# A cross-attention and fp4 feed-forward kernel: the down projection as three f32r products in place of one f32 product

## Chip, cores and metric

One core of a Trainium2 chip runs the whole program. The metric is the device time of one execution in microseconds (us), lower is better. A second number for the same execution is the span of its trace, from the first to the last instruction of the program.

## What is computed

For x (8, 512, 256) and ctx (8, 512, 256): layer norm, cross-attention with 16 heads of 16 and an additive bias and mask, a residual, then layer norm and a feed-forward of width 704 whose activations and weights are all rounded to fp4 in blocks of 16, and a residual. The change is in the last product.

```python
def fp4_quant_dequant(x):                       # blocks of 16 along the last dim
    scale = jnp.max(jnp.abs(xb), axis=-1, keepdims=True) / 6.0
    q = _GRID[jnp.searchsorted(_MID, jnp.abs(xb / scale))] * jnp.sign(xb) * scale

def fp4_linear(x, w):
    return jnp.einsum('bsk,nk->bsn', fp4_quant_dequant(x), fp4_quant_dequant(w))

x = x + attention(layernorm(x), ctx, ctx, bias, mask)
x2 = layernorm(x)
gate, y = fp4_linear(x2, w_gate), fp4_linear(x2, w_up)
h = jax.nn.silu(gate) * y
out = x + fp4_linear(h, w_down)                 # (4096, 704) times (704, 256)
```

## The kernel before

The program is written by hand, engine by engine: each of the blocks `sync`, `gpsimd`, `scalar`, `vector` and `tensor` is the instruction stream of one engine, and the streams meet only at counted semaphores. No scheduler moves anything, so an instruction waits for its semaphore and for all that stands before it on its engine.

**Attention, about 25 to 690 us.** The outer loop runs over 8 batch elements, each in 32 steps (`S_`). A step makes two score tiles of 128 x 512 (`scores`, L1331). VectorE takes each one from PSUM, adds the bias and finds the row's maximum in one instruction (`less_scores`, L1089), and writes it to `prob`, a ring of 13 buffers (`RING`). GpSimd or ScalarE subtracts the maximum (`less_max`). TensorE transposes the tile four steps later (`T_LAG`, 8 tiles), ScalarE takes the exponential, and TensorE multiplies by the values. Between the tiles lie the projections of the next octet of heads, and, in the last batch element, the nine pieces in which the feed-forward weights are made: VectorE, GpSimd and ScalarE round a piece, TensorE transposes it (`make_weights`), ScalarE copies it to SBUF (`take_weights`, L764 to L767 for w_down). For gate and up the copy goes to an f32r buffer `w_gu_high`, and VectorE stores what the rounding to f32r lost in `w_gu_low` (`weights_low`, L1031). For w_down the copy goes to an f32 buffer `w_dnT`, and `weights_low` returns without doing anything.

**Feed-forward, about 690 to 929 us.** 32 row tiles of 128 rows go through a software pipeline (`ffn_step` on each engine, iteration n). In iteration n TensorE does, in this order: the six transposes of the rounded h of tile n-3 into `ps_h` (L1233 by way of the helper `transposes`); the gate and up products of tile n (L1567 to L1569, three f32r products for each of two chunks and three column ranges, 18 in all); two transposes of the rounded x of tile n+1 into `ps_x` (L1578), which leave the accumulation open; the first three chunks of the down product of tile n-3 (L1584); one product of minus the identity with the high part of x (`neg_ident`, L1594), which leaves x minus its high part in `ps_x`; and the last three chunks of the down product. The down product has six chunks of the 704 (padded to 768) rows of h, stationary `f_hqT` and moving `w_dnT`, both f32; each `matmul` call appears in the trace as two MATMUL records.

ScalarE does in iteration n: the copy of `ps_h` to `f_hqT` for tile n-3 (L903), two steps of the normalisation of tile n+3 (L874, L878), silu of tile n (L909), an absolute value for x of tile n+2 (L896), the high part of x of tile n+1 (`x_high`, L884), an absolute value for h of tile n-1 (L918), and the low part of x of tile n+1 (`x_low`, L889).

VectorE does the rounding steps and the last addition (L1197), and GpSimd scales the rounded h (L701).

Of the kernel before, what the change touches and what calls it, by code (L numbers as in the profile page):

```python
# [21 lines left out]
P = 128  # L22
# [19 lines left out]
def xattn_ffn(nc, x, ctx, bias, mask, w_in, b_in, w_out, b_out, w_gate, w_up, w_down, out):  # L42
# [19 lines left out]
    TILES = 2 * STEPS  # L62
    T_LAG = 4
    V_LAG = 8
    RING = 13
    VW = D + 1

    x_v = x.rearrange("b (t p) e -> p (b t) e", p=P)
# [5 lines left out]
    with cx:  # L74
        def sb(name, shape, dt=F32):
            return cx.enter_context(nc.sbuf_tensor(name, shape, dt))

        def sem(name):
            return cx.enter_context(nc.semaphore(name))
# [5 lines left out]
        eps_t = sb("eps_t", [P, NT])  # L85
        neg_half = sb("neg_half", [P, NT])

        att = sb("att", [P, 28352])
        used = [0]

        def cut(*shape):
            n = 1
            for s in shape:
                n *= s
            a = att[:, used[0]:used[0] + n]
            used[0] += n
            assert used[0] <= att.shape[1], used[0]
            names = "abcd"[:len(shape)]
            if len(shape) == 1:
                return a  # L100
            return a.rearrange(f"p ({' '.join(names)}) -> p {' '.join(names)}",
                               **{k: s for k, s in zip(names[1:], shape[1:])})
# [16 lines left out]
        O_sb = cut(S)  # L119
        O_n = cut(NT, E)  # L120
        oT = cut(EC, S)
        at_w_dn = used[0]
        w_dnT = cut(IC, E)
        w_outT = cut(EC, E)
        bv_bc = cut(E)
        bo_bc = cut(E)


        w_qT = att[:, at_w_dn:at_w_dn + EC * E].rearrange("p (c e) -> p c e", c=EC)

        w_nat = probT.rearrange("p a b c d -> p (a b c d)")[:, 0:8 * E].rearrange("p (c e) -> p c e", c=8)

# [27 lines left out]
        kv_hl = sb("kv_hl", [P, 4 * EC * S], F32R)  # L160
        ctxT_high, ctxT_low, w_kv_high, w_kv_low = (
            kv_hl[:, i * EC * S:(i + 1) * EC * S].rearrange("p (c s) -> p c s", c=EC) for i in range(4))
        assert 2 * E == S and EC * GU <= 4 * EC * S
        w_gu_low = kv_hl[:, 0:EC * GU].rearrange("p (c n) -> p c n", c=EC)

        WPC = 512
# [27 lines left out]
        def lows_of(z):  # L194


            return sum(1 for i in range(z) if piece_rows(i)[0] < 2)
        used[0] = at_bias
        f_xc = cut(E)
        f_xn = cut(2, E)  # L200
# [13 lines left out]
        f_hu = cut(I)  # L214

        f_hq = cut(2, IC * P)
        f_hqT = cut(2, IC, P)
        f_out = cut(2, E)
        assert used[0] <= at_bias

        psum = cx.enter_context(nc.psum_tensor("psum", [P, 8, 512], F32))
        ps_score, ps_O = psum[:, 0:3, :], psum[:, 6, :]
# [58 lines left out]
        fhy_ready, fha_ready = sem("fhy_ready"), sem("fha_ready")  # L281
        fhu_ready, fhd_ready, fhq_ready = sem("fhu_ready"), sem("fhd_ready"), sem("fhq_ready")
        fhT_ready, fhT_taken = sem("fhT_ready"), sem("fhT_taken")
        fdn_ready, fout_ready = sem("fdn_ready"), sem("fout_ready")
        stored = [sem(f"stored{i}") for i in range(2)]

# [273 lines left out]
        def _(pool):  # L560
# [77 lines left out]
            for o in range(EC):  # L638
                pool.memset(vv[:, o, :, 0:8 * VW].rearrange("p c (h m) -> p c h m", m=VW)[:, :, :, D:VW], 1.0).then_inc(vv_zero, 1)

            pool.memset(w_dnT[:, IC - 1, :], 0.0).then_inc(vv_zero, 1)
            low_k(0)
            low_q(0)
            for tt in range(NT):
# [63 lines left out]
        def _(act):  # L708
# [44 lines left out]
            def take_weights(z, bank):  # L753

                act.wait_ge(gwT_ready, z + 1)
                src = bank.rearrange("p (c n) -> p c n", c=2)
                g, m = piece_rows(z)
                if g < 2:

                    act.wait_ge(score_ready, TILES * (N_OCT - 1))  # L760
                    cols = min(2 * P, I - m * P)
                    act.activation(w_gu_high[:, :, g * I + m * P:g * I + m * P + cols], src[:, :, 0:cols], ACT.Copy).then_inc(gwT_taken, 1)
                elif m < IC - 2:
                    act.activation(w_dnT[:, m:m + 2, :], src, ACT.Copy).then_inc(gwT_taken, 1)  # L764
                else:
                    act.activation(w_dnT[:, m, :], src[:, 0, :], ACT.Copy)
                    act.activation(w_dnT[0:ILAST, m + 1, :], src[0:ILAST, 1, :], ACT.Copy).then_inc(gwT_taken, 1)  # L767

            def exp_tile(n, s, r):

# [127 lines left out]
            def ffn_step(n, par):  # L898
                m = n - 3
                if live(m):  # L900
                    act.wait_ge(fhT_ready, m + 1)
                    wait(act, fdn_ready, m - 1)
                    act.activation(f_hqT[:, 1 - par, :, :].rearrange("p c t -> p (c t)"), ps_h[:, 0:IC * P], ACT.Copy).then_inc(fhT_taken, 1)  # L903
                x_norm(n + 3, 1 - par)
                m = n
                if live(m):
                    act.wait_ge(fgate_ready, m + 1)
                    wait(act, fh_ready, m - 1)
                    act.activation(f_sil[:, par, :], ps_gu[:, 0:I], ACT.Silu).then_inc(fsil_ready, 1)  # L909
                if live(n + 2):  # L910
                    x_abs(n + 2, par)
                if live(n + 1):
                    x_high(n + 1, 1 - par)
                m = n - 1
                if live(m):
                    act.wait_ge(fhy_ready, m + 1)
                    wait(act, fhd_ready, m)
                    act.activation(f_ha, f_hy[:, 1 - par, :], ACT.Abs, scale=PULL).then_inc(fha_ready, 1)  # L918
                if live(n + 1):
                    x_low(n + 1, 1 - par)  # L920
            batches(act, body)
# [20 lines left out]
        def _(dve):  # L942
# [288 lines left out]
        def _(pe):  # L1231
# [317 lines left out]
            def ffn_step(n, par):  # L1549
                m = n - 3  # L1550
                if live(m):
                    if isinstance(m, int) and m == 0:
                        pe.wait_ge(o_taken, 2 * B)
                    pe.wait_ge(fhq_ready, m + 1)
                    wait(pe, fhT_taken, m)
                    for c in range(IC):
                        last = transposes(ps_h[:, c * P:(c + 1) * P], f_hq[:, 1 - par, c * P:(c + 1) * P])
                    last.then_inc(fhT_ready, 1)
                m = n
                if live(m):  # L1560
                    pe.wait_ge(fxlow_ready, m + 1)
                    wait(pe, fh_ready, m)
                    for c0 in range(0, GU, 512):
                        c1 = min(c0 + 512, GU)

                        for c in range(EC):
                            pe.matmul(ps_gu[:, c0:c1], f_xqT_high[:, par, c, :], w_gu_high[:, c, c0:c1], start=c == 0, stop=False)  # L1567
                            pe.matmul(ps_gu[:, c0:c1], f_xqT_high[:, par, c, :], w_gu_low[:, c, c0:c1], start=False, stop=False)  # L1568
                            last = pe.matmul(ps_gu[:, c0:c1], f_xqT_low[:, par, c, :], w_gu_high[:, c, c0:c1], start=False, stop=c == EC - 1)  # L1569
                        if c0 < I <= c1:  # L1570
                            last.then_inc(fgate_ready, 1)
                    last.then_inc(fgu_ready, 1)
                m = n + 1
                if live(m):
                    pe.wait_ge(fxq_ready, m + 1)
                    wait(pe, fxlow_ready, m)
                    for c in range(EC):
                        last = pe.matmul(ps_x[:, c * P:(c + 1) * P], f_xq[:, 1 - par, c * P:(c + 1) * P], ident[:, :],  # L1578
                                         start=c == 0, stop=False, is_transpose=True, skip_group_check=True)
# [67 lines left out]
```

## Time and profile before

| | |
|---|---|
| median of 3 runs | 929.09 us (928.99 to 929.43) |
| the profiled execution, its own time | 930.9 us |
| span of its trace | 928.9 us |
| busy: TensorE / VectorE / ScalarE / GpSimd | 95% / 76% / 67% / 58% of the span |
| granted TensorE clock, mean of the core | 0.993 of full speed |
| one period of the feed-forward, from one row tile to the next | 7.41 us |

The busy share of TensorE is that of its matmul records, which overlap one another: a record lasts longer than the time after which the next one starts. So costs on TensorE are read from start to start, and not from the mean duration.

### The profile page before, as it was taken

What the parts mean: (1) busy time and instruction counts of PE and PEld (TensorE: products, weight loads), DVE (VectorE), ACT (ScalarE), POOL (GpSimd) and SP (SyncE); (2) the same over time, 40 slices, a digit from 0 to 9 for tenths busy, and PEclk for the clock granted to TensorE, in tenths of its full rate; (3) what the DMA queues carried; (4) which work ended last, traced back from release to release, by engine and by line L of the source; (5) the groups of instructions that cost most, each with busy time, mean ns of one, the idle gap of its engine ahead of it and who ended that gap; (6) DMA issues with size and microseconds to landing.
All of it is one profiled execution on the core that took longest, in us unless ns stands there. A gap on an engine that the chain in (4) does not pass through costs nothing.

```text
span 928.9 us, 20211 instructions
## 1 busy us (share of the span) xinstructions
PE 883.6 (95%) x6772; PEld 706.7 (76%) x6772; DVE 710.6 (76%) x1866; ACT 617.8 (67%) x1119; POOL 534.8 (58%) x501
## 2 busy tenths in 40 slices
PE   5699999999999999999999999999889999999997
PEld 5577777787777777777787777777568888888886
DVE  3868678677677776776776679899579999989984
ACT  2377677777677776777776777787755555555542
POOL 5677867776696687677678557875203222222222
PEclk9799999999999999999999999999999999999999
DMA  6577334442442534344243343610000000000000
GB/s 193 150 221 205 113 72 126 103 117 71 114 116 60 146 86 102 98 100 132 74 115 103 72 134 73 174 35 1 1 1 12 18 18 19 21 17 17 18 18 29
DMA packets 50796, 76.50 MB, mean 82 GB/s; under 512 B 5264, under 2 KB 22032, under 8 KB 50704
## 3 DMA queue, kind: packets, MB, share of 16 engines
q1 hardware_dynamic: 50448, 75.06, 29.9%
q8 instruction: 52, 0.85, 0.4%
q10 hardware_dynamic: 256, 0.26, 0.1%
q14 instruction: 40, 0.33, 0.1%
HBM read 45.16 MB, written 29.36 MB: 80 GB/s over the span
## 4 chain that ended last, share of the span: by engine, by line
PE 79%; ACT 6%; issue 6%; DVE 4%; POOL 2%; DMA 2%; SPq 1%; ACTq 0%; DVEq 0%
PE psum L1233 26%; PE psum L1377 11%; PE psum L1331 11%; PE psum L1584 9%; PE psum L1569 4%; PE psum L1568 4%; PE psum L1567 4%; PE psum L1295 3%; PE psum L1255 2%; ACT att L776 2%; DVE att L1089 2%; PE psum L1261 2%; ACT att L783 1%; PE psum L1272 1%; ACT att L727 1%
## 5 line engine op out<-in xcount | busy, mean ns | idle before, releaser
L1089 DVE CUSTOM_DVE_ANT_0 att<-psum,att 128x512 f32<-128x512 f32 x512 | 341.7, 686 | 143.3 <-PE psum L1331 141.4
L618 POOL TENSOR_TENSOR att<-att,neg_max 128x512 f32<-128x512 f32 x308 | 322.4, 1057 | 172.8 <-DVE neg_max L1089 170.4
L1233 PE MATMUL psum<-ident,att 128*128 128x128 f32 x2576 | 380.8, 276 | 25.2 <-ACT att L776 8.2
L1233 PEld LDWEIGHTS psum<-ident,att 128*128 128x128 f32 x2576 | 311.6, 142 | 93.0 <-ACT att L776 30.2
L776 ACT ACTIVATE att<-psum 128x512 f32<-128x512 f32 x512 | 298.3, 599 | 117.7 <-PE psum L1233 113.4
L1331 PE MATMUL psum<-stack 128*128 128x512 f32 x512 | 251.2, 492 | 10.5 <-DMA stack<-q_hl 7.2
L783 ACT ACTIVATE att<-att,neg_max 128x512 f32<-128x512 f32 x204 | 147.2, 722 | 13.4 <-DVE neg_max L1089 13.4
L701 POOL TENSOR_TENSOR att<-att 128x704 f32<-128x704 f32 x32 | 61.8, 1931 | 162.8 <-DVE att L1211 162.8
L1331 PEld LDWEIGHTS psum<-stack 128*128 128x128 f32 x512 | 97.8, 191 | 43.9 <-issue 32.3
L1377 PE MATMUL psum<-att 128*32 128x256 f32 x2048 | 123.8, 382 | 0.0
L1584 PE MATMUL psum<-att 128*128 128x256 f32 x384 | 91.7, 380 | 2.7 <-ACT att L903 2.7
L1377 PEld LDWEIGHTS psum<-att 128*32 128x32 f32 x2048 | 60.0, 109 | 44.0 <-issue 8.6
L1584 PEld LDWEIGHTS psum<-att 128*128 128x128 f32 x384 | 68.4, 190 | 10.9 <-ACT att L903 3.4
L1567 PE MATMUL psum<-stack,q_hl 128*128 128x512 f32 (+1 forms) x192 | 74.4, 387 | 0.6 <-ACT q_hl L889 0.6
L1569 PE MATMUL psum<-stack,q_hl 128*128 128x512 f32 (+1 forms) x192 | 72.1, 376 | 0.0
L1568 PE MATMUL psum<-kv_hl,q_hl 128*128 128x512 f32 (+1 forms) x192 | 71.9, 375 | 0.0
L903 ACT ACTIVATE att<-psum 128x768 f32<-128x768 f32 x32 | 26.0, 814 | 53.4 <-PE psum L1233 53.4
L909 ACT ACTIVATE att<-psum 128x704 f32<-128x704 f32 x32 | 24.3, 760 | 38.1 <-PE psum L1569 38.1
L1160 DVE TENSOR_TENSOR att<-att,psum 128x704 f32<-128x704 f32 x32 | 28.4, 888 | 23.2 <-PE psum L1569 22.8
L1089 DVE DVE_READ_ACCUMULATOR2_ANT neg_max<- 128x1 f32 x512 | 42.1, 82 | 0.0
L602 POOL TENSOR_TENSOR att<-att 128x512 f32<-128x512 f32 x32 | 41.4, 1298 | 0.0
L1567 PEld LDWEIGHTS psum<-stack,q_hl 128*128 128x128 f32 x192 | 36.1, 188 | 6.3 <-ACT q_hl L889 0.8
(104 smaller groups left out, 1066.3 us busy)
## 6 DMA issues: line engine op xcount, KB each, us to landing
stack<-qk_planes SPq DMA_DIRECT2D x124, 192.0 KB, 3.9
qk_planes<-k_hl SPq DMA_DIRECT2D x48, 256.0 KB
qk_planes<-q_hl SPq DMA_DIRECT2D x48, 256.0 KB
att<-in_fside_1xSxS_dram SPq DMA_DIRECT2D x32, 256.0 KB, 2.8
att<-in_ctx_dram SPq DMA_DIRECT2D x8, 512.0 KB, 7.4
out_dram<-att SPq DMA_DIRECT2D x32, 128.0 KB, 1.7
x<-in_x_dram SPq DMA_DIRECT2D x1, 2560.0 KB, 13.5
x<-in_x_dram SPq DMA_DIRECT2D x3, 512.0 KB, 6.5
```

Of the source, the lines that this page charges most:

```text
L618: pool.tensor_tensor(prob[:, slot, :], prob[:, slot, :], neg_max[:, slot:slot + 1].to_broadcast([P, S]), ALU.subtract).then_inc(less_pool, 1)
L701: pool.tensor_tensor(blocks(f_hq[:, par, 0:I]), blocks(f_hu), spread(f_s[:, 1 - par, 0:NHB], NHB), ALU.mult).then_inc(fhq_ready, 1)
L776: act.activation(probT[:, u % 2, 2 * kk + r, :, (tt % 2) * P:(tt % 2 + 1) * P], src.rearrange("p (c t) -> p c t", c=SC), ACT.Exp, scale=1. ...
L783: act.activation(prob[:, slot, :], prob[:, slot, :], ACT.Identity, bias=neg_max[:, slot:slot + 1], scale=-1.0).then_inc(less_act, 1)
L1089: dve.tensor_tensor_reduce(out=prob[:, slot, :], in0=ps_score[:, SCORE_BANK[2 * S_ + r], :], in1=bias_m[:, tt, :], scale=-1.0, scalar=BIG, ...
L1233: return pe.transpose(out_, in_, ident[:, :])
L1331: pe.matmul(ps_score[:, SCORE_BANK[j], :], stack[:, quad % SLOTS, kk, r, tt * P:(tt + 1) * P], stack[:, quad % SLOTS, kk, 2, :], start=Tru ...
L1377: last = pe.matmul(ps_O[32 * j:32 * j + 32, half * 2 * P:(half + 1) * 2 * P], vv[:, o, c, col:col + 2 * D], probT[:, u % 2, j, c, :], star ...
L1567: pe.matmul(ps_gu[:, c0:c1], f_xqT_high[:, par, c, :], w_gu_high[:, c, c0:c1], start=c == 0, stop=False)
L1568: pe.matmul(ps_gu[:, c0:c1], f_xqT_high[:, par, c, :], w_gu_low[:, c, c0:c1], start=False, stop=False)
L1569: last = pe.matmul(ps_gu[:, c0:c1], f_xqT_low[:, par, c, :], w_gu_high[:, c, c0:c1], start=False, stop=c == EC - 1)
L1584: last = pe.matmul(ps_y[:, 1 - par, :], f_hqT[:, 1 - par, c, :], w_dnT[:, c, :], start=c == 0, stop=c == IC - 1)
```

## The change

The down product is done as gate and up are: h and w_down are each split in a high f32r part and the low part that is left, and the product is high by high, high by low, and low by high, 18 f32r products in place of 6 f32 ones.

- `weights_low` now stores the low parts of w_down too, three pieces, in the place of `k_hl` and behind `kv_hl`; `lows_of` counts them, so that `weights_free` on TensorE waits for them as well.
- The transposes of h leave their accumulation open. Two products of minus the identity with h's high part leave h's low part in `ps_h`. ScalarE copies it a second time (`fhlow_ready`), behind the absolute value of h and ahead of `x_low`.
- The buffers move: `f_hqT` becomes a part of `stack`, `w_dnT` a part of `kv_hl`; the ring has 12 buffers.

```diff
-    RING = 13
+    RING = 12
...
-            pool.memset(w_dnT[:, IC - 1, :], 0.0).then_inc(vv_zero, 1)
+            pool.memset(kv_hl[:, 4 * EC * S:].bitcast(F32), 0.0).then_inc(vv_zero, 1)
...
         def lows_of(z):
-            return sum(1 for i in range(z) if piece_rows(i)[0] < 2)
+            return z
...
             def weights_low(z, bank):
                 g, m = piece_rows(z)
-                if g == 2:
-                    return
                 dve.wait_ge(gwT_taken, z + 1)
+                if g == 2:
+                    src = bank.rearrange("p (c n) -> p c n", c=2)
+                    if m < IC - 2:
+                        dve.wait_ge(k_plane, 48 * N_OCT)
+                        dve.tensor_tensor(w_dn_low4[:, m:m + 2, :], src, w_dn_high[:, m:m + 2, :].bitcast(F32), ALU.subtract).then_inc(gw_low, 1)
+                    else:
+                        dve.tensor_tensor(w_dn_low2[:, 0, :], src[:, 0, :], w_dn_high[:, m, :].bitcast(F32), ALU.subtract)
+                        dve.tensor_tensor(w_dn_low2[0:ILAST, 1, :], src[0:ILAST, 1, :], w_dn_high[0:ILAST, m + 1, :].bitcast(F32),
+                                          ALU.subtract).then_inc(gw_low, 1)
+                    return
...
 # ScalarE, ffn_step
-                    act.activation(f_hqT[:, 1 - par, :, :].rearrange("p c t -> p (c t)"), ps_h[:, 0:IC * P], ACT.Copy).then_inc(fhT_taken, 1)
+                    act.activation(hqT_hl[:, 1 - par, 0, :], ps_h[:, 0:IC * P], ACT.Copy).then_inc(fhT_taken, 1)
...
                     act.activation(f_ha, f_hy[:, 1 - par, :], ACT.Abs, scale=PULL).then_inc(fha_ready, 1)
+                if live(n - 3):
+                    act.wait_ge(fhlow_made, n - 2)
+                    act.activation(hqT_hl[:, 1 - par, 1, :], ps_h[:, 0:IC * P], ACT.Copy).then_inc(fhlow_ready, 1)
                 if live(n + 1):
                     x_low(n + 1, 1 - par)
...
 # TensorE, ffn_step
                     for c in range(IC):
-                        last = transposes(ps_h[:, c * P:(c + 1) * P], f_hq[:, 1 - par, c * P:(c + 1) * P])
+                        last = pe.matmul(ps_h[:, c * P:(c + 1) * P], f_hq[:, 1 - par, c * P:(c + 1) * P], ident[:, :],
+                                         start=c % 4 == 0, stop=False, is_transpose=True, skip_group_check=True)
...
-                def down(m, chunks):
-                    for c in chunks:
-                        last = pe.matmul(ps_y[:, 1 - par, :], f_hqT[:, 1 - par, c, :], w_dnT[:, c, :],
-                                         start=c == 0, stop=c == IC - 1)
-                    return last
-
                 if live(n - 3):
                     pe.wait_ge(fhT_taken, n - 2)
+                    for c0, c1 in ((0, 512), (512, IC * P)):
+                        last = pe.matmul(ps_h[:, c0:c1], neg_ident[:, :], hqT_hl[:, 1 - par, 0, c0:c1], start=False, stop=True,
+                                         skip_group_check=True)
+                    last.then_inc(fhlow_made, 1)
                     wait(pe, fout_ready, n - 3)
-                    down(n - 3, range(0, IC // 2))
+                    for c in range(IC):
+                        high = hqT_hl[:, 1 - par, 0, c * P:(c + 1) * P]
+                        pe.matmul(ps_y[:, 1 - par, :], high, w_dn_high[:, c, :], start=c == 0, stop=False)
+                        pe.matmul(ps_y[:, 1 - par, :], high, w_dn_low(c), start=False, stop=False)
                 if live(m):
                     pe.wait_ge(fxT_taken, m + 1)
                     pe.matmul(ps_x[:, 0:E], neg_ident[:, :], f_xqT_high[:, 1 - par, :, :], start=False, stop=True,
                               skip_group_check=True).then_inc(fxlow_made, 1)
                 if live(n - 3):
-                    down(n - 3, range(IC // 2, IC)).then_inc(fdn_ready, 1)
+                    pe.wait_ge(fhlow_ready, n - 2)
+                    for c in range(IC):
+                        last = pe.matmul(ps_y[:, 1 - par, :], hqT_hl[:, 1 - par, 1, c * P:(c + 1) * P], w_dn_high[:, c, :],
+                                         start=False, stop=c == IC - 1)
+                    last.then_inc(fdn_ready, 1)
```

TensorE in the feed-forward, from the transposes of x of the next tile to the transposes of h of the tile after, before:

```order
L1578 MATMUL psum<-ident,att 128x128 x2
L1584 MATMUL psum<-att 128x256 x3
L1594 MATMUL psum<-q_hl,neg_ident 128x256
L1584 MATMUL psum<-att 128x256 x3
L1233 MATMUL psum<-ident,att 128x128 x6
```

and now (the pair L1617, L1618 stands six times, its low part of w_down from `k_hl` four times and from `kv_hl` twice):

```order
L1603 MATMUL psum<-ident,att 128x128 x2
L1611 MATMUL psum<-stack,neg_ident 128x512
L1611 MATMUL psum<-stack,neg_ident 128x256
L1617 MATMUL psum<-kv_hl,stack 128x256
L1618 MATMUL psum<-k_hl,stack 128x256
...
L1617 MATMUL psum<-kv_hl,stack 128x256
L1618 MATMUL psum<-kv_hl,stack 128x256
L1621 MATMUL psum<-q_hl,neg_ident 128x256
L1626 MATMUL psum<-kv_hl,stack 128x256 x6
L1581 MATMUL psum<-ident,att 128x128 x6
```

Twenty f32r products stand where six f32 ones stood, and the product for x's low part (L1594, now L1621) has moved behind fourteen of them, ahead of the last six.

ScalarE in one iteration of the same loop, before and then now:

```order
L903 ACTIVATE att<-psum 128x768
L874 ACTIVATE att<-x,neg_mean 128x256
L878 ACTIVATE att<-att,rstd 128x256
L909 ACTIVATE att<-psum 128x704
L896 ACTIVATE att<-att 128x256
L884 ACTIVATE q_hl<-psum 128x256
L918 ACTIVATE att<-att 128x704
L889 ACTIVATE q_hl<-psum 128x256
```

```order
L915 ACTIVATE stack<-psum 128x768
L884 ACTIVATE att<-x,neg_mean 128x256
L888 ACTIVATE att<-att,rstd 128x256
L921 ACTIVATE att<-psum 128x704
L906 ACTIVATE att<-att 128x256
L894 ACTIVATE q_hl<-psum 128x256
L930 ACTIVATE att<-att 128x704
L933 ACTIVATE stack<-psum 128x768
L899 ACTIVATE q_hl<-psum 128x256
```

The new copy (L933) stands third after the copy of x's high part: behind it (L894) and the absolute value of h (L930).

## Rows read from the trace of the kernel before

**Rows 1.** Busy time by stage: us, busy PE PEld DVE ACT POOL (x records), clock, DMA, GB/s
```profile
600.00:620.00 20.00, 18.05 (x168) 13.53 (x164) 19.78 (x51) 17.06 (x33) 16.02 (x17) 1.00 0.30 77
620.00:640.00 20.00, 19.64 (x171) 15.27 (x171) 19.01 (x49) 16.02 (x30) 12.33 (x14) 1.00 0.01 2
703.00:911.00 208.00, 208.00 (x1096) 182.52 (x1096) 187.12 (x387) 115.86 (x217) 56.33 (x29) 1.00 0.05 18
911.00:928.90 17.90, 12.50 (x63) 9.97 (x61) 7.68 (x14) 3.22 (x4) 3.35 (x2) 1.00 0.09 30
```

**Rows 2.** The chain that ended last, in one period: start us, us, what
```profile
784.58 1.30 PE psum L1584 x6
785.99 1.29 PE psum L1584 x6
787.29 0.66 PE psum L1233 x6
...
791.99 1.30 PE psum L1584 x6
```

**Rows 3.** Timeline, PE and weight loads: start us, us, engine line, out<-in, count
```profile
37.04 0.42 PEld L1272 LDWEIGHTS psum<-kv_hl 128*128 128x128 f32 x3
37.39 0.19 PEld L1331 LDWEIGHTS psum<-stack 128*128 128x128 f32 x1
...
788.48 0.39 PE L1567 MATMUL psum<-stack,q_hl 128*128 128x512 f32 x1
...
789.17 0.39 PE L1567 MATMUL psum<-stack,q_hl 128*128 128x512 f32 x1
```

**Rows 4.** Timeline of one period, PE and ACT, with idle time and its releaser
```profile
784.20 0.38 PE L1578 MATMUL psum<-ident,att 128*128 128x128 f32 x2
784.42 1.46 PE L1584 MATMUL psum<-att 128*128 128x256 f32 x6
784.62 0.38 ACT L884 ACTIVATE q_hl<-psum 128x256 fp32r<-128x256 f32 x1 [0.22 <-PE psum L1578]
784.90 0.78 ACT L918 ACTIVATE att<-att 128x704 f32<-128x704 f32 x1
786.03 0.38 ACT L889 ACTIVATE q_hl<-psum 128x256 fp32r<-128x256 f32 x1 [0.35 <-PE psum L1594]
787.12 0.82 PE L1233 MATMUL psum<-ident,att 128*128 128x128 f32 x6
787.98 0.81 ACT L903 ACTIVATE att<-psum 128x768 f32<-128x768 f32 x1 [1.57 <-PE psum L1233]
788.69 0.50 ACT L874 ACTIVATE att<-x,neg_mean 128x256 f32 x1
```

**Rows 5.** Timeline at the stage's start: TensorE resumes after a wait for ScalarE
```profile
691.65 0.38 ACT L889 ACTIVATE q_hl<-psum 128x256 fp32r<-128x256 f32 x1
...
692.08 0.50 PE L1567 MATMUL psum<-stack,q_hl 128*128 128x512 f32 x1 [0.57 <-ACT q_hl L889]
...
692.42 0.40 PE L1568 MATMUL psum<-kv_hl,q_hl 128*128 128x512 f32 x1
```

**Rows 6.** Timeline of the last tile
```profile
922.48 0.81 ACT L903 ACTIVATE att<-psum 128x768 f32<-128x768 f32 x1 [3.60 <-PE psum L1233]
923.34 2.86 PE L1584 MATMUL psum<-att 128*128 128x256 f32 x12 [0.90 <-ACT att L903]
926.24 0.42 DVE L1197 TENSOR_TENSOR att<-psum,x 128x256 f32<-128x256 f32 x1 [3.99 <-PE psum L1584]
```

**Rows 7.** Timeline of VectorE in the last batch element
```profile
603.26 0.41 DVE L989 COPY att<-psum 128x256 f32<-128x256 f32 x1
603.59 0.67 DVE L1089 CUSTOM_DVE_ANT_0 att<-psum,att 128x512 f32<-128x512 f32 x1
...
626.89 0.68 DVE L1031 TENSOR_TENSOR kv_hl<-psum,stack 128x512 fp32r<-128x512 f32 x1
627.49 0.68 DVE L1089 CUSTOM_DVE_ANT_0 att<-psum,att 128x512 f32<-128x512 f32 x1
```

**Rows 8.** Timeline of GpSimd at the start of the program
```profile
7.80 1.11 POOL L636 MEMSET att<- 128x1216 f32 x1
...
9.09 0.31 POOL L641 MEMSET att<- 128x256 f32 x1
...
16.78 1.27 POOL L596 TENSOR_TENSOR k_hl<-att,k_hl 128x512 fp32r<-128x512 f32 x1 [7.38 <-DVE k_hl L972]
```

More of the change, by code:

```diff
@@ L86, in xattn_ffn @@
         neg_half = sb("neg_half", [P, NT])
-        att = sb("att", [P, 28352])
+        att = sb("att", [P, 26816])
         used = [0]
@@ L121, in xattn_ffn @@
         oT = cut(EC, S)
-        at_w_dn = used[0]
-        w_dnT = cut(IC, E)
+        w_qT = cut(EC, E)
         w_outT = cut(EC, E)
@@ L126, in xattn_ffn @@
         bo_bc = cut(E)
-        w_qT = att[:, at_w_dn:at_w_dn + EC * E].rearrange("p (c e) -> p c e", c=EC)
         w_nat = probT.rearrange("p a b c d -> p (a b c d)")[:, 0:8 * E].rearrange("p (c e) -> p c e", c=8)
@@ L158, in xattn_ffn, with w_dn_low @@
         w_gu_high = stack[:, (2 * N_OCT - 3) % SLOTS, :, :, :].rearrange("p x k s -> p (x k s)")[:, 0:EC * GU].rearrange("p (c n) -> p c n", c=EC)
-        kv_hl = sb("kv_hl", [P, 4 * EC * S], F32R)
+        AT_DN = EC * GU
+        kv_hl = sb("kv_hl", [P, AT_DN + (IC + 2) * E], F32R)
         ctxT_high, ctxT_low, w_kv_high, w_kv_low = (
             kv_hl[:, i * EC * S:(i + 1) * EC * S].rearrange("p (c s) -> p c s", c=EC) for i in range(4))
-        assert 2 * E == S and EC * GU <= 4 * EC * S
+        assert 2 * E == S and 4 * EC * S <= AT_DN + (IC + 2) * E
+        w_dn_high = kv_hl[:, AT_DN:AT_DN + IC * E].rearrange("p (c e) -> p c e", c=IC)
+        w_dn_low2 = kv_hl[:, AT_DN + IC * E:].rearrange("p (c e) -> p c e", c=2)
+        w_dn_low4 = k_hl.rearrange("p a s -> p (a s)").rearrange("p (c e) -> p c e", c=IC - 2)
+        def w_dn_low(c):
+            return w_dn_low4[:, c, :] if c < IC - 2 else w_dn_low2[:, c - IC + 2, :]
         w_gu_low = kv_hl[:, 0:EC * GU].rearrange("p (c n) -> p c n", c=EC)
@@ L216, in xattn_ffn @@
         f_hq = cut(2, IC * P)
-        f_hqT = cut(2, IC, P)
         f_out = cut(2, E)
         assert used[0] <= at_bias
+        assert 4 * IC * P == 6 * S
+        hqT_hl = stack[:, (2 * N_OCT - 1) % SLOTS, :, :, :].rearrange("p x k s -> p (x k s)").rearrange(
+            "p (i j n) -> p i j n", i=2, j=2)
         psum = cx.enter_context(nc.psum_tensor("psum", [P, 8, 512], F32))
@@ L283, in xattn_ffn @@
         fhT_ready, fhT_taken = sem("fhT_ready"), sem("fhT_taken")
+        fhlow_made, fhlow_ready = sem("fhlow_made"), sem("fhlow_ready")
         fdn_ready, fout_ready = sem("fdn_ready"), sem("fout_ready")
@@ L763, in take_weights @@
                 elif m < IC - 2:
-                    act.activation(w_dnT[:, m:m + 2, :], src, ACT.Copy).then_inc(gwT_taken, 1)
+                    act.activation(w_dn_high[:, m:m + 2, :], src, ACT.Copy).then_inc(gwT_taken, 1)
                 else:
-                    act.activation(w_dnT[:, m, :], src[:, 0, :], ACT.Copy)
-                    act.activation(w_dnT[0:ILAST, m + 1, :], src[0:ILAST, 1, :], ACT.Copy).then_inc(gwT_taken, 1)
+                    act.activation(w_dn_high[:, m, :], src[:, 0, :], ACT.Copy)
+                    act.activation(w_dn_high[0:ILAST, m + 1, :], src[0:ILAST, 1, :], ACT.Copy).then_inc(gwT_taken, 1)
             def exp_tile(n, s, r):
@@ L902, in ffn_step @@
                     wait(act, fdn_ready, m - 1)
-                    act.activation(f_hqT[:, 1 - par, :, :].rearrange("p c t -> p (c t)"), ps_h[:, 0:IC * P], ACT.Copy).then_inc(fhT_taken, 1)
+                    if isinstance(m, int) and m == 0:
+                        act.wait_ge(score_ready, TILES * N_OCT)
+                    act.activation(hqT_hl[:, 1 - par, 0, :], ps_h[:, 0:IC * P], ACT.Copy).then_inc(fhT_taken, 1)
                 x_norm(n + 3, 1 - par)
@@ L1554, in ffn_step @@
                     pe.wait_ge(fhq_ready, m + 1)
-                    wait(pe, fhT_taken, m)
+                    wait(pe, fhlow_ready, m)
                     for c in range(IC):
-                        last = transposes(ps_h[:, c * P:(c + 1) * P], f_hq[:, 1 - par, c * P:(c + 1) * P])
+                        last = pe.matmul(ps_h[:, c * P:(c + 1) * P], f_hq[:, 1 - par, c * P:(c + 1) * P], ident[:, :],
+                                         start=c % 4 == 0, stop=False, is_transpose=True, skip_group_check=True)
                     last.then_inc(fhT_ready, 1)
```

## Prediction

> **What bounds the kernel.** I first read the busy time by stage [rows 1]. In the steady part of the feed-forward, 703 to 911 us, TensorE has a record open in all 208.00 us, while VectorE is busy 187.12 and ScalarE 115.86. In the attention stage before it, the stretch 600 to 620 us is different: there VectorE is the full one (19.78 of 20.00) and TensorE is not (18.05); in the next 20 us TensorE is nearly full again. Then I read the chain that ended last [rows 2]. In a period of the feed-forward every link is TensorE's, with no wait between: 784.58 to 791.99 us is one period, 7.41 us, in which the down product takes 1.30 + 1.29 = 2.59 us and the one product of minus the identity the 0.11 to 0.12 us between its halves. So in this stage a change on TensorE counts at its full size, once for each row tile, as long as TensorE finds its inputs ready. The timeline of one period [rows 4] then tells which inputs could be late.
>
> **TensorE's own work.** I price by the distance from start to start. Three f32r weight loads for products of 256 columns begin at 37.04 and the load behind them at 37.39: 0.35 / 3 = 0.117 us for each product [rows 3]. Of 512 columns, three take 789.17 - 788.48 = 0.69, so 0.23 each [rows 3]. The f32 down product takes 2.59 / 6 = 0.43 for each chunk [rows 2].
>
> - Removed in a period: 6 f32 chunks, 2.59.
> - Added: minus the identity by 512 and by 256 columns, 0.23 + 0.12 = 0.35; 18 f32r products, 18 x 0.117 = 2.11. Together 2.46.
> - Net: -0.13 us a tile, if nothing waits. Over 32 tiles that would be -4.2 us.
>
> What speaks against these prices is a rule of the weight path. The rows show that the load is hidden: an f32r load record lasts 0.19 us, and yet the products behind it come every 0.117 us [rows 3]. The Trainium skill, page "TensorE: Matmul & The Clock Gate", Part 3, section "The mechanism", says that a weight load runs beside matmuls in flight only when it goes to another row group, and all products here use all the rows. By that rule each of the 20 loads would stand ahead of its product; the trace disagrees, and I go by the rows. What it would give is the third rival.
>
> **The new wait.** The last six products need h's low part, which ScalarE copies from PSUM. Nothing in the trace of before shows this wait, so I build the chain from the rows of one period. Let T be the start of the two transposes of x, 784.20 [rows 4].
>
> - ScalarE's copy of x's high part waits for those transposes and starts at T + 0.42 (784.62). The absolute value of h stands behind it and starts at T + 0.70 (784.90), lasts 0.78 and ends at T + 1.48 [rows 4].
> - The new copy stands behind that. In a row without a wait ScalarE's next record starts about 0.10 before the end of the last: 787.98 + 0.81 = 788.79, next start 788.69 [rows 4]. So it starts at T + 1.38. It reads what L903 reads, 128 x 768 from PSUM, so it lasts 0.81 [rows 4] and ends at T + 2.19. Its own input is ready before: the two products of minus the identity start at T + 0.22 and take 0.35, and a product's record ends some 0.2 later.
> - TensorE resumes late after a wait: ScalarE's L889 ends at 691.65 + 0.38 = 692.03, L1567 starts at 692.08, and the next product only 0.34 later in place of 0.23 [rows 5]. That is 0.05 + 0.11 = 0.16. So the six count from T + 2.35, and end at T + 2.35 + 6 x 0.117 = T + 3.05.
> - Without the wait TensorE would be there at T + 0.22 + 0.35 + 12 x 0.117 + 0.12 = T + 2.09, and the six would end at T + 2.79. Before, the transposes of h started at T + 2.92 (787.12) [rows 4].
>
> So the wait ends last: TensorE stands for 0.26 us, the saving of 0.13 is gone, and a period grows by 3.05 - 2.92 = 0.13 us. From the first down product at 703 us to the last iteration that also transposes x there are 28 such periods: **+3.6 us**. The bounds of this term: with a restart that costs only the 0.05, it is +0.02 a tile, +0.6 us; with a copy that takes 0.1 more because it writes f32r, +0.23 a tile, +6.4 us. The two x copies write f32r from PSUM at 0.38 for 256 columns [rows 4], which speaks for no extra cost, so I take the middle.
>
> In the last four tiles no x is transposed, ScalarE is early, and the saving stays. For the last one, from the end of the high copy (923.29) to the last addition (926.24) it took 2.95 [rows 6]; now 0.16 + 0.35 + 12 x 0.117 + 6 x 0.117 = 2.61, and some 0.2 until the result is seen, 2.81. Four tiles at -0.14: **-0.6 us**.
>
> **x's low part** is delayed on both engines: its product now starts at T + 1.97, and its copy, which started at T + 1.83 (786.03) [rows 4], follows the new one and that product, at about T + 2.4, and ends at T + 2.8. It is needed by the gate products at T + 3.05 + 0.66. It stays hidden by 0.9 us. ScalarE's next copy (L903) comes behind the transposes of h and had 1.57 us of idle ahead of it [rows 4]; the new copy of 0.81 and the shift fit in.
>
> **The attention stage.** VectorE gets the low parts of w_down, in steps 9, 11 and 13 of the last batch element, which lie in 600 to 620 us. Two are of 128 x 512: from L1031 at 626.89 to the next at 627.49, 0.60 each [rows 7]. The third is two instructions of 256 columns, 0.33 each by L989 [rows 7]. Together 1.86. VectorE is full there [rows 1], with two score tiles in each step behind it, and TensorE, GpSimd and ScalarE wait for those: **+1.9 us**. At least 0.3, if the 0.22 of idle and TensorE's own queue take up the most; at most 2.8, if VectorE also stands for ScalarE's copy of a piece (in order on both engines) 0.3 us three times. TensorE's wait for the low part before it reuses the bank adds none of its own, since VectorE has two more score tiles to work on meanwhile.
>
> **Edits at nothing.** The ring of twelve: VectorE may write tile t once tile t-12 is transposed. TensorE issues the transposes of t-9 before the scores of t, and VectorE waits for those scores first, so the wait is over when it comes to it; this holds down to nine. GpSimd's memset grows from 256 to 768 columns, about 0.7 in place of 0.31 us by the one of 1216 in 1.11, and 7.38 us of idle follow it [rows 8]. No DMA is added or moved. The clock is 1.00 in all these stretches [rows 1], and TensorE's gaps of a fraction of a microsecond are like those of the attention stage, which has 1.00 too.
>
> **Sum.** +3.6 - 0.6 + 1.9 = +4.9 us. Against the profiled execution's own time, 930.9, that is 935.8. The median of the runs was 929.1, 1.8 lower, so I predict 934.0. A difference of under 0.2% (1.9 us) is about what a measurement of this kernel can't tell from none.
>
> **Rivals.**
>
> 1. *The wait is hidden (faster).* If the low copy is seen by T + 2.09, TensorE never stands, and the periods give -0.13 x 28 - 0.6 = -4.2; with +1.9 from attention it is -2.3: 926.8. It decides at 0.15 us: the copy's end at T + 2.19, seen 0.05 later, must come 0.15 earlier. For it speaks that the chain is made of five small numbers; against it that each is read in this very loop, and that ScalarE's order is fixed, with 0.78 + 0.81 us behind the x copy. Chance 0.08.
> 2. *The wait about eats the saving.* Restart at 0.05 and half of VectorE's work absorbed: +0.6 - 0.6 + 0.9 = +0.9, 930.0. Chance 0.12.
> 3. *Weight loads are exposed.* A period has 20 loads in place of 12 and each costs its 0.19: +1.52 - 0.13 = +1.4 us, times 32, +44, with attention 975. The spacing of 0.117 in rows 3 is against it. This is the rule of the Trainium skill named above. Chance 0.01.
>
> The forecast, slower by 0.2% or more, keeps 0.79. Its own range is 929.1 + 0.6 - 0.6 + 1.9 = 931.0 to 929.1 + 6.4 - 0.6 + 2.8 = 937.7. To leave out no more than 2 in 10 the range reaches down through the second rival to both lower bounds, 929.1 + 0.6 - 0.6 + 0.3: 929.4 to 937.7. Slower takes the forecast and the third rival, 0.80; same 0.12; faster 0.08.
>
> **What would show it.** In the profile of the changed kernel the period should be 7.54 us; the first of the six last products (L1626) should have idle ahead of it, released by ScalarE's L933, of 0.1 to 0.3 us, 28 times; L933 should start within a record of L930's end and last 0.81; the twelve products of L1617 and L1618 should take 1.40. Of attention: the stage should end about 1.9 us later, with VectorE as full as before in 600 to 622 us. If L1626 never waits, rival 1 holds. If VectorE's low parts don't move the end of attention, the sum is 2 us too high.

## The result and the profile after

The changed kernel takes 935.44 us (median of 4 runs, 934.74 to 937.73) against 929.08 before (928.99 to 929.43): +6.4 us, ratio 1.007 with a 95% interval of 1.0052 to 1.0087. It is slower, inside the predicted range, and 1.4 us above the predicted 934.0.

The stages of the changed kernel by the windows of [rows 1] (us, busy PE PEld DVE ACT POOL with records, clock, DMA share, GB/s). They are moved back by 1.4 us, since this execution came to its first score tile 1.4 us earlier than the one before (see below):

```profile
598.60:618.60 20.00, 17.21 (x159) 12.79 (x148) 19.68 (x48) 14.90 (x29) 14.38 (x15) 1.00 0.30 77
618.60:638.60 20.00, 18.62 (x161) 14.28 (x162) 19.02 (x49) 16.02 (x30) 12.32 (x14) 1.00 0.01 2
```

VectorE is as full as before there, and TensorE has lost 0.84 us of busy time in the first stretch (18.05 before) and 1.02 in the second (19.64 before). One period of the feed-forward in the timeline, PE and ACT, which answers to [rows 4]:

```profile
786.33 0.38 PE L1603 MATMUL psum<-ident,att 128*128 128x128 f32 x2
786.47 0.59 PE L1611 MATMUL psum<-stack,neg_ident 128*128 128x512 f32 x2
786.75 0.38 ACT L894 ACTIVATE q_hl<-psum 128x256 fp32r<-128x256 f32 x1 [0.22 <-PE psum L1603]
786.90 0.28 PE L1617 MATMUL psum<-kv_hl,stack 128*128 128x256 f32 x1
787.02 0.28 PE L1618 MATMUL psum<-k_hl,stack 128*128 128x256 f32 x1
787.03 0.79 ACT L930 ACTIVATE att<-att 128x704 f32<-128x704 f32 x1
...
787.71 0.80 ACT L933 ACTIVATE stack<-psum 128x768 fp32r<-128x768 f32 x1
...
788.34 0.28 PE L1621 MATMUL psum<-q_hl,neg_ident 128*128 128x256 f32 x1
...
788.56 0.98 PE L1626 MATMUL psum<-kv_hl,stack 128*128 128x256 f32 x6
788.65 0.38 ACT L899 ACTIVATE q_hl<-psum 128x256 fp32r<-128x256 f32 x1
...
789.38 0.82 PE L1581 MATMUL psum<-ident,att 128*128 128x128 f32 x6
...
793.86 0.38 PE L1603 MATMUL psum<-ident,att 128*128 128x128 f32 x2
```

With T = 786.33 the transposes of h start at T + 3.05, where they started at T + 2.92 before, and a period is 793.86 - 786.33 = 7.53 us. The low copy L933 ends at 788.51, and the first of the last six products starts 0.05 later.

A period has two parts. From the transposes of x to those of h, where all the products lie that the change adds, removes or moves, it takes 2.92 us before and 3.05 now. The rest, the transposes of h and the gate and up products, is 4.48 to 4.49 us in both.

To see where the time went I cut the trace at landmarks that every kernel here has: VectorE's 1st, 465th and 481st instruction that adds the bias (L1089, now L1113; the 465th to the 480th hold the w_down pieces), ScalarE's third and last silu, and the end. Lengths in us between them:

| kernel | 1st to 465th | 465th to 481st | to third silu | 28 periods and the one before | last silu to end |
|---|---|---|---|---|---|
| before | 571.25 | 20.03 | 72.78 | 214.12 | 19.67 |
| changed | 571.05 | 22.39 | 72.77 | 217.65 | 20.45 |
| difference | -0.20 | +2.36 | -0.01 | +3.53 | +0.78 |

That is +6.5 us. The two profiled executions differ by only 935.96 - 930.9 = 5.1 us, since the first bias instruction came at 31.07 us in the one and at 29.67 in the other. The rows (of before, then of the changed kernel):

```profile
31.07 0.63 DVE L1089 CUSTOM_DVE_ANT_0 att<-psum,att 128x512 f32<-128x512 f32 x1
```

```profile
29.67 0.63 DVE L1113 CUSTOM_DVE_ANT_0 att<-psum,att 128x512 f32<-128x512 f32 x1
```

The medians, 6.4 us apart, agree with the landmarks.

The first tile of the tail, after the last gate and up product, in the changed kernel:

```profile
918.61 0.61 PE L1611 MATMUL psum<-stack,neg_ident 128*128 128x512 f32 x2 [0.90 <-ACT stack L915]
...
919.16 0.89 DVE L1239 TENSOR_TENSOR att<-att 128x704 f32<-128x704 f32 x1
...
920.08 0.79 ACT L930 ACTIVATE att<-att 128x704 f32<-128x704 f32 x1 [1.52 <-DVE att L1239]
...
920.78 0.79 ACT L933 ACTIVATE stack<-psum 128x768 fp32r<-128x768 f32 x1
921.62 0.98 PE L1626 MATMUL psum<-kv_hl,stack 128*128 128x256 f32 x6 [0.97 <-ACT stack L933]
```

The low copy could have started at about 919.3. It stood behind the absolute value of h (L930) of another tile, and that waited for VectorE's L1239. TensorE is idle for 0.97 us. The prediction did not have this wait.

### The profile page after: what moved, and what is told of

It is laid out like the page before. It is cut to its first block, busy times and chain, and to the rows that moved or that the text cites. A ratio compares the mean times of both kernels' runs of the same rounds, so it can differ in the third digit from the quotient of the medians.

```text
span 934.0 us, 20731 instructions
## 1 busy us (share of the span) xinstructions
PE 885.2 (95%) x7028; PEld 714.5 (76%) x7028; DVE 712.8 (76%) x1870; ACT 639.9 (69%) x1151; POOL 534.4 (57%) x501
## 4 chain that ended last, share of the span: by engine, by line
PE 78%; issue 6%; ACT 6%; DVE 5%; POOL 2%; DMA 2%; SPq 1%; DVEq 0%; ACTq 0%
PE psum L1257 23%; PE psum L1401 11%; PE psum L1355 11%; PE psum L1594 4%; PE psum L1593 4%; PE psum L1592 4%; PE psum L1626 3%; PE psum L1319 3%; PE psum L1279 2%; PE psum L1617 2%; PE psum L1618 2%; PE psum L1581 2%; ACT att L786 2%; DVE att L1113 2%; PE psum L1285 2%
## 5 line engine op out<-in xcount | busy, mean ns | idle before, releaser
L1113 DVE CUSTOM_DVE_ANT_0 att<-psum,att 128x512 f32<-128x512 f32 x512 | 341.7, 687 | 143.1 <-PE psum L1355 141.4
L786 ACT ACTIVATE att<-psum 128x512 f32<-128x512 f32 x512 | 297.8, 598 | 117.8 <-PE psum L1257 113.5
L1257 PE MATMUL psum<-ident,att 128*128 128x128 f32 x2384 | 353.6, 275 | 25.3 <-ACT att L786 8.5
L1257 PEld LDWEIGHTS psum<-ident,att 128*128 128x128 f32 x2384 | 288.2, 141 | 89.3 <-ACT att L786 30.5
L1594 PE MATMUL psum<-stack,q_hl 128*128 128x512 f32 (+1 forms) x192 | 72.1, 376 | 0.0
L915 ACT ACTIVATE stack<-psum 128x768 fp32r<-128x768 f32 x32 | 26.0, 813 | 40.9 <-PE psum L1581 40.9
L1617 PE MATMUL psum<-kv_hl,stack 128*128 128x256 f32 x192 | 47.5, 283 | 0.0
L1113 DVE DVE_READ_ACCUMULATOR2_ANT neg_max<- 128x1 f32 x512 | 42.3, 83 | 0.0
L749 ACT ACTIVATE att<-psum 128x512 f32<-128x512 f32 x32 | 19.1, 598 | 32.8 <-PE psum L1401 32.8
```

Source lines behind the costliest of these rows:

```text
L786: act.activation(probT[:, u % 2, 2 * kk + r, :, (tt % 2) * P:(tt % 2 + 1) * P], src.rearrange("p (c t) -> p c t", c=SC), ACT.Exp, scale=1. ...
L1113: dve.tensor_tensor_reduce(out=prob[:, slot, :], in0=ps_score[:, SCORE_BANK[2 * S_ + r], :], in1=bias_m[:, tt, :], scale=-1.0, scalar=BIG, ...
L1257: return pe.transpose(out_, in_, ident[:, :])
L1617: pe.matmul(ps_y[:, 1 - par, :], high, w_dn_high[:, c, :], start=c == 0, stop=False)
```

## The experiments

Each kernel was compared with the kernel before on the chip it ran on. The first four shared one chip (before: 930.66, 23 runs), the last two another (before: 930.87, 13 runs). The landmarks of all six, in the columns of the table above:

| kernel | 1st to 465th | 465th to 481st | to third silu | 28 periods and the one before | last silu to end |
|---|---|---|---|---|---|
| copy first | 571.22 | 22.40 | 72.79 | 211.32 | 19.42 |
| lows alone | 571.05 | 22.40 | 72.78 | 214.10 | 19.66 |
| tail only | 571.56 | 23.31 | 72.79 | 216.99 | 19.40 |
| split later | 571.51 | 20.02 | 72.79 | 211.33 | 19.39 |
| ring of 13 | 571.07 | 22.39 | 72.80 | 216.93 | 20.45 |
| split only | 569.91 | 20.02 | 72.77 | 217.61 | 20.43 |

### Copy first: h's low part ahead of the absolute value of h

```diff
                 if live(n + 1):
                     x_high(n + 1, 1 - par)
+                if live(n - 3):
+                    act.wait_ge(fhlow_made, n - 2)
+                    act.activation(hqT_hl[:, 1 - par, 1, :], ps_h[:, 0:IC * P], ACT.Copy).then_inc(fhlow_ready, 1)
                 m = n - 1
                 if live(m):
                     act.wait_ge(fhy_ready, m + 1)
                     wait(act, fhd_ready, m)
                     act.activation(f_ha, f_hy[:, 1 - par, :], ACT.Abs, scale=PULL).then_inc(fha_ready, 1)
-                if live(n - 3):
-                    act.wait_ge(fhlow_made, n - 2)
-                    act.activation(hqT_hl[:, 1 - par, 1, :], ps_h[:, 0:IC * P], ACT.Copy).then_inc(fhlow_ready, 1)
```

> The changed kernel with ScalarE's copy of h's low part moved ahead of the absolute value of h in its order, nothing else. My theory: in the steady part the last six products wait because that copy stands behind the absolute value of h, and in the tail because that absolute value itself waits for VectorE. Then the wait before the last six products is gone in every tile, a period falls from 7.53 to about 7.33 us (28 times, -5.5 us), the tail loses the 1.0 us stand plus a little, and the time is about 928.6 us. Rival: the twenty f32r products cost more than the six f32 ones by themselves (weight loads, spacing), and the wait only shows where TensorE would have been late anyway: then the period stays at 7.53 and the time at 935.4.

Measured: 929.43 us, ratio to before 0.9994 (0.9985 to 1.0002). By its interval it can't be told from the kernel before. One period in its timeline:

```profile
783.87 0.38 PE L1603 MATMUL psum<-ident,att 128*128 128x128 f32 x2
...
784.29 0.38 ACT L894 ACTIVATE q_hl<-psum 128x256 fp32r<-128x256 f32 x1 [0.22 <-PE psum L1603]
784.64 0.81 ACT L928 ACTIVATE stack<-psum 128x768 fp32r<-128x768 f32 x1
785.35 0.78 ACT L933 ACTIVATE att<-att 128x704 f32<-128x704 f32 x1
785.88 0.28 PE L1621 MATMUL psum<-q_hl,neg_ident 128*128 128x256 f32 x1
...
786.00 0.88 PE L1626 MATMUL psum<-kv_hl,stack 128*128 128x256 f32 x6
786.20 0.39 ACT L899 ACTIVATE q_hl<-psum 128x256 fp32r<-128x256 f32 x1
...
786.72 0.82 PE L1581 MATMUL psum<-ident,att 128*128 128x128 f32 x6
```

The copy (L928) ends at 785.45, 0.55 us before it is needed. The six products follow L1621 by one spacing of 0.12, and their group takes 0.88 where it took 0.98. The transposes of h start at T + 2.85, 0.07 earlier than before the change and 0.20 earlier than with it. By the landmarks the loop is 2.80 us shorter than that of before, 0.10 for each of 28 periods, and 6.33 shorter than that of the change. Not all of that is the moved line's. The edited part of a period gives 0.075 against before (2.1 us in 28 periods) and 0.20 against the change (5.5 us). The rest, some 0.025 us a period, lies in the transposes of h and the gate and up products, where the two kernels have the same products; the same difference shows between two kernels that have the same loop (see the end). The rival falls even so: without the wait twenty f32r products are cheaper than six f32 ones, by 0.075 us a tile. What is left against before is attention's 2.4, and the two nearly cancel.

### Lows alone: VectorE's four instructions in the kernel before

```diff
         def lows_of(z):
-            return sum(1 for i in range(z) if piece_rows(i)[0] < 2)
+            return z
...
                 if g == 2:
+                    dve.wait_ge(gwT_taken, z + 1)
+                    ... as in the change, subtracting w_dnT ...
                     return
```

> The kernel before with one part of the change alone: VectorE's low parts of w_down (three pieces, four instructions) and TensorE's wait for them before it reuses the bank; the results are stored but not used, and the feed-forward is that of before. My theory: VectorE is full in that stretch, and two waits in it stretch the cost, so +2.3 to +2.4 us, 931.4, as the traces of the two kernels drift apart there. Rival: the drift came from elsewhere in the change (ring of twelve, moved buffers), and the four instructions are hidden: 929.1. A third value: only the bare 1.9 us of my sum, 931.0.

Measured: 932.51 us, ratio 1.0025 (1.0014 to 1.0037), which is 1.3 to 3.4 us. The landmarks place it: 22.40 us in the stretch of the w_down pieces, as in the change, and 20.03 without; every other length is within 0.2 us of that of before. The whole loss in attention is that of these four instructions. Its interval alone would not tell 1.9 from 2.4; the trace does.

### Tail only: the copy first only after the last gate and up product

```diff
+                tail = isinstance(n, int) and n >= ROWS
+                if tail and live(n - 3):
+                    act.wait_ge(fhlow_made, n - 2)
+                    act.activation(hqT_hl[:, 1 - par, 1, :], ps_h[:, 0:IC * P], ACT.Copy).then_inc(fhlow_ready, 1)
                 m = n - 1
...
-                if live(n - 3):
+                if live(n - 3) and not tail:
```

> The changed kernel with the copy of h's low part ahead of the absolute value of h only in the iterations after the last gate and up product (the last three tiles); the loop is as in the change. My theory: in the first of them the copy waits behind an absolute value that waits for VectorE's scaling of the last h, and this costs about 1.1 us; so -1.1 to -1.3 us, 934.2, with the period unchanged at 7.53. Rival: the longer tail comes from the products of minus the identity and the restarts, which this doesn't touch: 935.4.

Measured: 934.84 us, ratio 1.0044 (1.0031 to 1.0057); the time by itself would not settle one microsecond. The landmark from the last silu to the end does: 19.40 us, where the change has 20.45 and before 19.67. So the wait in the tail costs 1.05, and without it the tail gains 0.27 on before. This execution's profile also shows something here that the others don't:

```profile
610.00:620.00 10.00, 9.27 (x76) 6.58 (x71) 8.48 (x21) 6.49 (x14) 4.32 (x7) 0.83 0.07 20
```

The granted clock is 0.83 over 610 to 620 us, that is the lower level of 1.2 GHz for a part of it, and the stretch takes 23.31 in place of 22.39. The kernels changed, copy first, lows alone and ring of 13 have the same instructions in this stretch, and their profiles have a clock of 1.00 there.

### Split later: w_down split by GpSimd once attention is over, with the copy first

```diff
-    RING = 12
+    RING = 10
...
+        w_dn_full4 = cut(IC - 2, E)
 # ScalarE, take_weights: as before the change, an f32 copy
-                    act.activation(w_dn_high[:, m:m + 2, :], src, ACT.Copy).then_inc(gwT_taken, 1)
+                    act.activation(w_dn_full4[:, m:m + 2, :], src, ACT.Copy).then_inc(gwT_taken, 1)
...
 # GpSimd, behind the batches
+            pool.wait_ge(k_plane, 48 * N_OCT)
+            pool.tensor_copy(w_dn_high[:, 0:IC - 2, :], w_dn_full4).then_inc(wdn_high, 1)
...
+            pool.wait_ge(wdn_high, 1)
+            pool.tensor_tensor(w_dn_low4, w_dn_full4, w_dn_high[:, 0:IC - 2, :].bitcast(F32), ALU.subtract).then_inc(wdn_split, 1)
...
             rstd2_of(B - 1)
 # VectorE: weights_low returns for g == 2, as before the change
...
 # TensorE, ffn_step
+                    if isinstance(n, int) and n == 3:
+                        pe.wait_ge(wdn_split, 2)
```

> The order of the first run (copy ahead of the absolute value), and the splitting of w_down moved off VectorE: ScalarE copies the f32 piece to SBUF as before the change, and GpSimd, idle from 660 us on, makes the high and low parts there; the ring has ten buffers to make room. My theory: the attention stage costs nothing more than before, so the time is that of the first run less 2.3: about 926.3 us, faster than before. It also says that a ring of ten costs nothing. Rival: GpSimd's extra 6 to 8 us delay its 1/std of the last batch element or the first tiles, or the small ring stalls VectorE: then 928 or more.

Measured: 927.31 us, ratio 0.9964 (0.9951 to 0.9976). It is faster than the kernel before by 0.2% to 0.5% (0.7 us of it, under 0.1%, is the 0.025 us a period named above), and than the change by some 1%. The timeline of GpSimd shows where the work went:

```profile
660.61 1.04 POOL L703 CAST kv_hl<-att 128x1024 fp32r<-128x1024 f32 x1
...
662.30 2.35 POOL L707 TENSOR_TENSOR k_hl<-att,kv_hl 128x1024 fp32r<-128x1024 f32 x1
...
665.30 0.72 POOL L710 TENSOR_TENSOR kv_hl<-att,kv_hl 64x256 fp32r<-64x256 f32 x1
689.08 0.20 POOL L589 TENSOR_TENSOR var_eps<-mean_var_b,eps_t 128x4 f32<-128x4 f32 x1 [23.06 <-DVE mean_var_b L1046]
```

The six instructions end at 666.0, and GpSimd then idles 23.06 us until VectorE has the variances (L1046) for its next one, so they lie in time in which it had nothing to do. The stretch of the pieces is back at 20.02, the loop at 211.33.

### Ring of 13 and split only

```diff
-    RING = 12
+    RING = 13
-        att = sb("att", [P, 26816])
+        att = sb("att", [P, 27328])
```

> The changed kernel with the ring back at thirteen buffers, nothing else. My theory: the smaller ring costs nothing, since TensorE's order has transposed tile t-9 before it makes the scores of tile t; so the same as the changed kernel, 935 us, and the attention stage as long to a tenth of a microsecond. Rival: the ring of twelve makes VectorE wait somewhere in 256 steps and part of the loss is its: then 1 to 3 us faster than the changed kernel.

Measured: 936.56 us, ratio 1.0067 (1.0051 to 1.0083), against 1.007 for the change. Its first 464 tiles take 571.07 us, those of the change 571.05. The ring of twelve costs nothing, and at ten buffers (571.51 and 569.91) nothing shows either. The execution with 569.91 was granted a clock of 0.97 over 30 to 50 us, and the others 0.77 to 0.88, which may be why it is shorter.

The last kernel is that of split later, with ScalarE's order of the change:

> The kernel of the fourth run (w_down split by GpSimd after attention, ring of ten) but with ScalarE's order of the change: the copy of h's low part behind the absolute value of h. It tells whether the two parts add up. My theory: attention as before the change (20.0 us where the change has 22.4), the loop at 7.53 us a period and the longer tail as in the change; so the changed kernel less 2.4, about 933 us, slower than before by some 4.3 us in the feed-forward alone. Rival: the loss in the loop depends on where w_down's parts were made or lie, and then the loop differs from that of the change.

Measured: 933.40 us, ratio 1.0038 (1.0024 to 1.0052), which is 2.2 to 4.8 us, +3.5 in the middle. The stretch of the pieces takes 20.02, the loop 217.61 (the change: 217.65), the tail 20.43. These three landmarks add up to +4.2 us against before, inside that interval and near the 4.3 expected. The loop does not ask where w_down's parts were made or lie.

## Why the prediction was right, and where its terms were off

The forecast, slower, came true, by two of its three terms. By the landmarks the loop's term was 0.1 too high, the tail's 1.4 too low and attention's 0.5 too low; with -0.2 from the time before the w_down pieces that is +6.5 in place of +4.9.

**TensorE's own work.** Predicted -0.13 us a tile without a wait. Copy first measures it: the transposes of h come 0.075 us earlier than before the change. (Its period is 0.10 shorter, but 0.025 of that lies in the transposes of h and the gate and up products, which are the same.) The spacing is 0.12 (L1617 at 786.90, L1618 at 787.02) and not 0.117, and nineteen of them make 0.06. Right mechanism, and a small slip in the third digit of a price, which took nearly half of a small difference of two large sums.

**The new wait.** Predicted: the copy starts at T + 1.38, lasts 0.81, ends at T + 2.19, and the period grows by 0.13 to 7.54. Measured: T + 1.38, 0.80, T + 2.18, +0.126, 7.53. TensorE stands 0.20 us (0.10 until the six start, 0.10 in their slower start) and not 0.26, because it arrives later by what the spacing adds; the two slips cancel in the period, since there ScalarE's chain sets the end. Copy first shows that this chain is the cause. The loop's term was +3.6, measured +3.5. The 0.10 of the slower start was forecast as 0.11, but the pair it was read from is a weak source: the same two products, L1567 and L1568, start 0.31 us apart in the kernel before where no wait stands ahead of them (787.70 and 788.01), in place of the 0.23 that I compared with. That the term came out right is in part luck.

```profile
787.70 0.47 PE L1567 MATMUL psum<-stack,q_hl 128*128 128x512 f32 x1
788.01 0.40 PE L1568 MATMUL psum<-kv_hl,q_hl 128*128 128x512 f32 x1
```

**The tail.** Predicted -0.6, measured +0.8. This is the step that failed: "In the last four tiles no x is transposed, ScalarE is early, and the saving stays." I took ScalarE to be early because the copy of x's high part was gone, and did not look at the instruction that then stands ahead of the low copy. It was the absolute value of h. Behind the last gate and up product ScalarE is idle 1.52 us ahead of that instruction, for VectorE's scaling of h (L1239), the low copy waits behind it, and TensorE is idle for 0.97 us: a wait that the prediction put at nothing. Tail only moves that term to -0.3, so the saving was half of what I took.

**Attention.** Predicted +1.9, measured +2.4. It is inside the bound of 2.8, but the bound was set for another reason: waits for ScalarE, and VectorE's idle time in this stretch grew by only 0.1. The four instructions cost what their rows said (0.60 + 0.60 + 0.34 + 0.34). The rest lies in their neighbours. In the changed kernel, with GpSimd's instruction (POOL) that was running when each of the changed ones began, or the last before it:

```profile
605.15 0.69 DVE L1049 TENSOR_TENSOR k_hl<-psum,kv_hl 128x512 fp32r<-128x512 f32 x1
...
605.70 1.27 POOL L621 TENSOR_TENSOR att<-att 128x512 f32<-128x512 f32 x1
...
606.13 1.40 DVE L1072 TENSOR_TENSOR att<-att,w_r 128x512 f32<-128x512 f32 x1
...
608.40 2.07 POOL L628 TENSOR_TENSOR att<-att,neg_max 128x512 f32<-128x512 f32 x2
...
611.70 0.68 DVE L1078 SCALAR_TENSOR_TENSOR att<-att 128x512 f32<-128x512 f32 x1
...
615.70 0.42 DVE L1051 TENSOR_TENSOR kv_hl<-psum,kv_hl 128x256 fp32r<-128x256 f32 x1
616.04 0.41 DVE L1052 TENSOR_TENSOR kv_hl<-psum,kv_hl 64x256 fp32r<-64x256 f32 x1
...
616.73 1.04 POOL L628 TENSOR_TENSOR att<-att,neg_max 128x512 f32<-128x512 f32 x1
616.74 1.57 DVE L1072 TENSOR_TENSOR att<-att,w_r 128x512 f32<-128x512 f32 x1
```

and the same instructions before:

```profile
606.30 1.04 POOL L618 TENSOR_TENSOR att<-att,neg_max 128x512 f32<-128x512 f32 x1 [0.51 <-DVE neg_max L1089]
...
607.12 0.76 DVE L1048 TENSOR_TENSOR att<-att,w_r 128x512 f32<-128x512 f32 x1
...
610.01 2.06 POOL L618 TENSOR_TENSOR att<-att,neg_max 128x512 f32<-128x512 f32 x2
...
611.47 1.14 DVE L1054 SCALAR_TENSOR_TENSOR att<-att 128x512 f32<-128x512 f32 x1
...
615.94 1.06 POOL L632 TENSOR_TENSOR att<-att,w_s 128x512 f32<-128x512 f32 x1
...
616.28 1.27 DVE L1048 TENSOR_TENSOR att<-att,w_r 128x512 f32<-128x512 f32 x1
```

One went from 0.76 to 1.40, one from 1.14 to 0.68, one from 1.27 to 1.57: +0.48 in sum, and 1.88 + 0.48 = 2.36. In both kernels the scaling of a piece takes between 0.75 and 1.58 us at the same size, by the moment at which it runs.

The traces tell what the moment decides. An instruction of VectorE on these lines that begins while a `TENSOR_TENSOR` of GpSimd is running ends 0.55 us after that one ends, however long it still runs. In the rows: GpSimd ends at 607.34 before and VectorE at 607.88; at 606.97 and 607.53 now; at 612.07 and 612.61 before, while now GpSimd was done at 610.47 and the instruction takes its 0.68. The three lines of a piece (L1048, L1054 and L1056 before) have 216 instructions in the eight traces. In 99 a `TENSOR_TENSOR` of GpSimd was running, and all 99 end 0.544 to 0.551 us behind it; the other 117 last 0.67 to 0.69 us, also where GpSimd was at a `TENSOR_SCALAR`. So the +0.48 is that VectorE's four new instructions shifted it against GpSimd. In split later and split only, which keep them off VectorE, the three lengths are back near 0.76, 1.14 and 1.27. No run moved GpSimd's instructions alone.

**Edits at nothing.** The ring and the layout cost nothing, as the runs show. x's low part stays hidden by 0.9 us as predicted: its copy ends at 789.03, and the first gate product starts at 789.95. That the weight loads stay hidden held too: 0.12 from product to product, in the change's own rows.

**A sign that was worded wrongly.** I had said that the first of the last six products would show idle time 28 times. It shows it three times:

```profile
its engine sat idle before it (us, times) until:
  ACT stack L933: 2.3, 3
```

The record of the product ahead lasts 0.28 us, and a stand of 0.20 hides under it. The wait shows in the starts (788.34 to 788.56 where the others follow by 0.12) and in the 0.98 of the group in place of 0.88.

## What to carry to other kernels

When an operation is split so that one engine hands its result to another and takes it back in the same iteration, build the chain by what stands ahead of the handed-over work in the other engine's order, and put that work first if something waits for it: here one moved line gave 0.20 us a tile. Do this again for the first and last iterations, where the instruction ahead may wait for something else: here that cost 1.0 us which the sum had put at nothing. When work is added to VectorE beside GpSimd, look at which of its instructions will then meet one of GpSimd's: here that added 0.5 us to 1.9. A preparation that runs once can go to an engine and a moment that are idle, which here took 2.4 us to nothing.

## What the runs showed of the hardware

- Executions of one loop differed by a constant: 28 periods and the one before took 217.65 and 217.61 us in two kernels with the order of the change, 216.93 and 216.99 in two others that have the same loop. That is 0.024 us a period. It lies in the transposes of h and the gate and up products: they take 4.48 or 4.49 us before, in the change, in lows alone and in split only, and 4.45 or 4.46 in the other four. The rows of the change, then of ring of 13:

```profile
789.38 0.82 PE L1581 MATMUL psum<-ident,att 128*128 128x128 f32 x6
...
793.86 0.38 PE L1603 MATMUL psum<-ident,att 128*128 128x128 f32 x2
```

```profile
790.67 0.81 PE L1581 MATMUL psum<-ident,att 128*128 128x128 f32 x6
...
795.12 0.38 PE L1603 MATMUL psum<-ident,att 128*128 128x128 f32 x2
```

  The granted clock is 1.00 in all eight over 700 to 900 us. Why the products follow closer in four of them stays open.
- A VectorE instruction with two inputs in SBUF that began while GpSimd ran a `TENSOR_TENSOR` ended 0.55 us after it, 99 times of 99. Its length was 0.75 to 1.58 us, by how much of GpSimd's was left, and it shows as a long record and not as idle time.
- The clock fell to its lower level for a part of 610 to 620 us in one profile of the five kernels with VectorE's four instructions, and the stretch took 0.9 us longer. A mean granted clock as low as 0.991 stands in 6 of 37 executions of these five kernels, and in none of 50 of the others (before, split later, split only), which would fit such a fall, though only one of the six has a trace. That the added waiting of TensorE brings it about is not shown.
- GpSimd made 1024 columns f32r from f32 in 1.04 us and subtracted 1024 columns in 2.35 us, while a subtraction of 512 columns took it 1.27 at the start of the program [rows 8].
